# A pre-norm linear-attention block on one core: the weights' opening in smaller pieces, and masks ahead of statistics in the last tiles

## What is computed

```python
x = x + attn(layernorm(x))       # 16 heads of 32
x = x + ffn(layernorm(x))        # 512 -> 512, operands rounded to fp8

# attn: q, k, v = split(x @ W_attn + b_attn);  q, k = elu(.) + 1
kv   = kv + k[:, None] * v[None, :]      # running sums over the tokens
ksum = ksum + k
y    = (q @ kv) / (q . ksum + 1e-6)
out  = y @ W_proj + b_proj
```

## Time and profile before

| | |
|---|---|
| median of 3 runs | 949.95 us (949.16, 949.95, 952.21) |
| profiled execution | 948.85 us, its span 947.1 us |
| PE busy | 918.2 us (97% of the span) |
| ACT busy | 745.6 us (79%) |
| DVE busy | 731.8 us (77%) |
| POOL busy | 641.3 us (68%) |
| granted clock of PE, mean | 0.999 |

### The profile page before, as it was taken

How to read it: one execution, slowest core, us unless ns; L and a number is a source line. 1 busy time by engine, 2 the same in 40 slices (tenths; PEclk the granted TensorE clock), 3 DMA queues, 4 the chain that set the end, 5 groups by cost and what they waited for, 6 DMA issues and landing times.

```text
span 947.1 us, 44776 instructions
## 1 busy us (share of the span) xinstructions
PE 918.2 (97%) x19470; PEld 490.5 (52%) x19532; DVE 731.8 (77%) x1404; ACT 745.6 (79%) x1358; POOL 641.3 (68%) x713
## 2 busy tenths in 40 slices
PE   5998999999999999999999999999999999999896
PEld 2455555555555555555555555555555555555454
DVE  6999879787777777778687687777778687676687
ACT  5788787877869688787877868788787878868874
POOL 5659877766767677676776667677676676764433
PEclk9999999999999999999999999999999999999999
DMA  8926564565464554565555465555555455462421
GB/s 268 143 41 109 109 119 103 97 119 97 95 122 100 98 116 104 96 114 105 95 114 107 91 116 106 89 118 108 92 114 112 89 114 110 90 103 59 76 69 59
DMA packets 252036, 99.12 MB, mean 105 GB/s; under 512 B 232384, under 2 KB 232640, under 8 KB 251840
## 3 DMA queue, kind: packets, MB, share of 16 engines
q1 hardware_dynamic: 251840, 96.25, 52.3%
HBM read 22.81 MB, written 16.78 MB: 42 GB/s over the span
## 4 chain that ended last, share of the span: by engine, by line
PE 90%; POOL 3%; issue 2%; ACT 2%; DVE 2%; SPq 1%; DMA 1%; ACTq 0%; POOLq 0%
PE R L235 77%; PE S L235 13%; POOL st L1029 1%; POOL xn L1031 1%; DMA x2t<-x2b 0%; ACT raw L477 0%; POOL xs L1076 0%; PE R L239 0%; DVE raw L739 0%; POOL raw L1062 0%; DMA xs<-in_L_attn_x 0%; ACT ktok L477 0%; SPq L1227 0%; DVE v L728 0%; ACT o L477 0%
## 5 line engine op out<-in xcount | busy, mean ns | idle before, releaser
L235 PE MATMUL R<-xt,wh 128*128 128x512 f16 x1024 | 306.2, 381 | 2.4 <-ACT wh L477 2.4
L716 DVE SCALAR_TENSOR_TENSOR qk<-qk,rel 128x512 f32<-128x512 f32 x128 | 112.8, 884 | 118.1 <-ACT rel L489 118.1
L477 ACT ACTIVATE raw<-qk 64x512 f32<-64x512 f32 x256 | 160.8, 628 | 48.9 <-PE S L235 45.7
L235 PE MATMUL R<-xt,wl 128*128 128x512 f16 x512 | 194.0, 380 | 0.0
L1083 POOL TENSOR_TENSOR yhl<-y,yhl 128x512 f16<-128x512 f32 x60 | 70.0, 1167 | 146.1 <-ACT yhl L477 146.1
L235 PE MATMUL R<-wh,xt 128*128 128x512 f16 x512 | 158.0, 379 | 0.0
L235 PEld LDWEIGHTS R<-xt,wh 128*128 128x128 f16 x1024 | 96.7, 98 | 116.0 <-DVE xt L882 2.6
L739 DVE TENSOR_TENSOR raw<-S,causal 64x1024 f32<-64x1024 f32 x128 | 155.9, 1218 | 0.9
L1029 POOL TENSOR_TENSOR st<-st,half 128x1 f32<-128x1 f32 x127 | 92.7, 730 | 90.6 <-DVE st L705 89.8
L235 PE MATMUL R<-wph,yt 128*128 128x512 f16 (+1 forms) x520 | 132.4, 377 | 3.9 <-ACT yt L477 1.9
L486 ACT ACTIVATE qk<-R,bqk,wm 128x512 f32<-128x512 f32 x128 | 98.9, 773 | 35.6 <-PE R L235 35.0
(11 more groups left out here) (108 smaller groups left out, 1364.8 us busy)
## 6 DMA issues: line engine op xcount, KB each, us to landing
xs<-in_L_attn_x SPq DMA_DIRECT2D x64, 256.0 KB, 3.1
out<-xs SPq DMA_DIRECT2D x63, 256.0 KB, 2.4
raw<-in_L_attn_W_attn SPq DMA_DIRECT2D x3, 1024.0 KB, 9.5
xs<-in_L_attn_W_proj SPq DMA_DIRECT2D x4, 256.0 KB
raw<-in_L_ffn_weight SPq DMA_DIRECT2D x1, 1024.0 KB, 17.0
raw<-raw SPq DMA_TRANSPOSE x63, 3.7
x2t<-x2b SPq DMA_TRANSPOSE x62, 2.5
xt<-xnhl SPq DMA_TRANSPOSE x60, 3.5
```

What stands on the lines that cost most here:

```text
L235: return e.matmul(out, a, b, start=start, stop=stop, skip_group_check=True)
L477: return e.activation(out, in_, ACT.Copy, **more)
L716: e.scalar_tensor_tensor(qk[j % 2][:, i, :], qk[j % 2][:, i, :], 1.0, rel[:, (u - 1) % 2, :], ALU.min, ALU.add).then_inc(s_phi, 1)
```

## The change

It has an opening part and an ending part. `W_attn` comes in four pieces instead of three (columns 0 to 256, 256 to 512, 512 to 1024, 1024 to 1536), each with its own size, spread and scale; `wh` and `wl` are made in eight parts, the first four of 128 columns. PE runs 16, 3 and 4 transposes that nobody reads (`warm`) among the first tiles' transposes, and `most(1)` inside the first product. `v_peak`, `v_scale`, `proj_scale`, `proj_weight` and `ffn_round` come later in the programs; `ffn_sum` moves from DVE to POOL; `add_bp` of tiles 8 to 23 moves, two at a time, to tiles 8 to 15. In the last tiles DVE makes `update` and the mask ahead of `ln2`, its residual `ffn` comes one tile later, POOL's `spread` comes ahead of `proj`, and PE's `ffn(28)` and `proj(30)` stand otherwise around `values(31)`.

```diff
+PIECES = ((0, 256), (256, 512), (512, 1024), (1024, 1536))
+PARTS = ((0, 128), (128, 256), (256, 384), (384, 512), (512, 768), (768, 1024), (1024, 1280), (1280, 1536))
...
# PE
                     if i == j == 0 and m == 8:
+                        most(1)
                         pe.wait_ge(s_wl, 1)
...
-            for m in range(4):
-                t1(m)
+            warm(16)
+            t1(0)
+            t1(1)
+            warm(3)
+            t1(2)
             most(0)
+            t1(3)
+            warm(4)
             for i in range(12):
                 proj_qkv(0, i)
-                if i in (0, 2, 11):
-                    most((0, 2, 11).index(i) + 1)
+                if i in (1, 4, 11):
+                    most((1, 4, 11).index(i) + 2)
...
                     if n == NT - 1:
-                        proj(n - 1, 0, 4)
+                        ffn(n - 3)
                     values(n)
...
                 if n == NT - 1:
-                    proj(n - 1, 4, 12)
+                    proj(n - 1, 0, 8)
                     t_y(n)
+                    proj(n - 1, 8, 12)
...
-                elif 2 <= n < NT - 1:
+                elif 2 <= n < NT - 2:
                     ffn(n - 2)
# ACT
             t1(1)
+            attn_size(0)
             t1(2)
-            attn_size(0)
             t1(3)
             attn_weight(0)
             attn_weight(1)
             attn_size(1)
-            phi(0, 0)
+            attn_size(2)
             attn_weight(2)
             attn_weight(3)
+            phi(0, 0)
+            attn_weight(4)
             phi(0, 1)
+            attn_weight(5)
...
                     if n == 0:
                         spread(n)
-                        proj_weight()
...
                     values(n)
                     if n == 0:
+                        proj_weight()
                         ahead(chunks(n)[1])
# DVE
             t1_parts(1)
+            scale(0)
             t1_parts(2)
-            scale(0)
             t1_parts(3)
             attn_weight(0)
             attn_weight(1)
-            v_peak()
             scale(1)
-            ln1(4)
-            attn_weight(2)
-            phi(0, 0)
-            attn_weight(3)
+            attn_weight(2)
+            attn_weight(3)
+            scale(2)
+            phi(0, 0)
+            ln1(4)
+            attn_weight(4)
             ln1(5)
             phi(0, 1)
-            scale(2)
+            v_peak()
+            attn_weight(5)
             phi(0, 2)
+            scale(3)
...
+            attn_weight(7)
             ln1(7)
...
             phi(0, 7)
+            v_scale()
             v_out(0, 0)
...
             update(0)
-            proj_scale()
...
+                    if n == 1:
+                        proj_weight()
+                        ahead(chunks(0)[1])
                     if n + 8 < NT:
                         ln1(n + 8)
                     if n == 0:
-                        proj_weight()
+                        proj_scale()
                     if n == 1:
-                        ffn_sum(0, 2)
+                        ffn_round()
...
                 if 1 <= n < NT:
                     proj(n - 1)
                 if n == NT - 1:
+                    ffn(n - 3)
                     t_y(n)
+                if n + 1 < NT and tail(n + 1):
+                    update(n + 1)
+                    scores(n + 1)
                 if 1 <= n < NT:
                     ln2(n - 1)
...
-                elif 2 <= n < NT - 1:
+                elif n < NT - 1 and tail(n - 1):
+                    ffn(n - 3)
+                elif n >= 2 and not tail(n):
                     ffn(n - 2)
# POOL, tile n
+            def ffn_sum(f):
+                pool.wait_ge(s_wfd, 3)
+                e.tensor_tensor(w_b[:, f, :], w_hi[:, f, :], w_lo[:, f, :], ALU.add).then_inc(s_wfs, 1)
...
+                    elif n < 8:
+                        add_bp(n)
+                    elif n < 16:
+                        add_bp(2 * n - 8)
+                        add_bp(2 * n - 7)
...
+                    if n == 1:
+                        ffn_sum(0)
+                        ffn_sum(1)
                     if n:
                         values(n)
+                    if n == 1:
+                        ffn_sum(2)
+                        ffn_sum(3)
+                if n + 1 < NT and tail(n + 1):
+                    spread(n + 1)
...
# SP
-                if n == 1:
-                    t_wf(0)
-                    t_wf(1)
                 if n + 2 < NT:
                     t_k(n + 2)
                 if n % 4 < 3 and n + 8 < NT:
                     t1(n + 8)
                 if n == 1:
+                    t_wf(0)
+                    t_wf(1)
                     t_y(n)
```

More of the change, by code:

```diff
@@ L141, in build @@
         Y = S[:, :, 4 * HALF:4 * HALF + 4 * W]
-        UN = [wm[:, 7 * i + 4:7 * i + 5] for i in range(4)]
-        UP = [wm[:, 7 * i + 5:7 * i + 6] for i in range(4)]
-        UN_V, UN_P = wm[:, 33:34], wm[:, 34:35]
+        UN = [wm[:, 7 * i + 4:7 * i + 5] for i in range(5)]
+        UP = [wm[:, 7 * i + 5:7 * i + 6] for i in range(5)]
+        UN_V, UN_P = wm[:, 41:42], wm[:, 42:43]
         raw_p = xs[:, NX - 4:NX, :]
@@ L162, in build @@
         s_out = [sem(f"xo{i}") for i in range(NX)]
-        s_wa = [sem(f"wa{i}") for i in range(3)]
+        s_wa = [sem(f"wa{i}") for i in range(4)]
         s_wf, s_wp, s_bqk, s_bva, s_bias = sem("wf"), sem("wp"), sem("bqk"), sem("bva"), sem("bias")
@@ L187, in build, with weights @@
         s_rs1, s_xn, s_rs2, s_x2, s_xb, s_x1b = sem("rs1"), sem("xn"), sem("rs2"), sem("x2"), sem("xb"), sem("x1b")
-        s_yl, s_blank, s_one, s_khl, s_near = sem("yl"), sem("blank"), sem("one"), sem("khl"), sem("near")
+        s_wfs, s_yl, s_blank, s_one, s_khl, s_near = sem("wfs"), sem("yl"), sem("blank"), sem("one"), sem("khl"), sem("near")
         bank = {}
+        def weights(first, end):
+            third, at = divmod(first, D)
+            return raw[:, third, :, at:at + end - first]
         def four(t):
@@ L500, in proj_size @@
                 act.wait_ge(s_wp, 64)
-                e.activation(wpl[:, :, :].bitcast(BF16), raw_p, ACT.Abs, accum_out=wm[:, 21:22]).then_inc(s_size, 1)
+                e.activation(wpl[:, :, :].bitcast(BF16), raw_p, ACT.Abs, accum_out=wm[:, 28:29]).then_inc(s_size, 1)
             def attn_weight(i):
[L504 to L507, removed]
+                piece = piece_of(PARTS[i][0])
+                act.wait_ge(s_up, piece + 1)
+                copy(wh[:, :, slice(*PARTS[i])], weights(*PARTS[i]), scale=UP[piece]).then_inc(s_wh, 1)
             def proj_weight():
-                act.wait_ge(s_up, 4)
-                copy(wph[:, :, :], raw_p, scale=UP[3]).then_inc(s_wph, 1)
+                act.wait_ge(s_up, 5)
+                copy(wph[:, :, :], raw_p, scale=UP[4]).then_inc(s_wph, 1)
             def ffn_half():
-                act.wait_ge(s_wl, 4)
+                act.wait_ge(s_wl, part_of(7) + 1)
                 act.wait_ge(s_wfc, 4)
@@ L933, in ffn_round @@
                                 saturate=False).then_inc(s_wfd, 1)
-            def ffn_sum(first, end):
-                dve.wait_ge(s_wfd, 3)
-                for f in range(first, end):
-                    e.tensor_tensor(w_b[:, f, :], w_hi[:, f, :], w_lo[:, f, :], ALU.add).then_inc(s_wfd, 1)
             e.memset(pair[:, :], 0.0).then_inc(s_pair, 1)
@@ L998, in _ @@
                         ffn_high()
-                        ffn_round()
-                        ahead(chunks(n)[1])
                 if 1 <= n < NT:
@@ L1008, in _ @@
                     last_proj()
-                if n + 1 < NT:
+                if n + 1 < NT and not tail(n + 1):
                     update(n + 1)
-                    if tail(n + 1):
-                        scores(n + 1)
-                if n == 1:
-                    ffn_sum(2, 4)
                 if n == NT:
@@ L1143, in _ @@
             ln1(4)
+            ln1(5)
             ln1_parts(4)
-            ln1(5)
             ln1_parts(5)
@@ L1173, in _ @@
                         ln1_parts(n + 8)
+                    if n == 1:
+                        ffn_sum(0)
+                        ffn_sum(1)
                     if n:
                         values(n)
-                    if 1 <= n < 8:
-                        add_bp(n)
+                    if n == 1:
[3 more added lines that the diff above has]
+                    spread(n + 1)
                 if n == NT:
@@ L1182, in _ @@
                     proj(n - 1)
-                if n + 1 < NT:
+                if n + 1 < NT and not tail(n + 1):
                     spread(n + 1)
                 if n == 0:
-                    add_bp(n + 8)
                     add_bp(n)
```

90 lines of the change are left out of this document (44 added, 46 removed).

## The result

The changed kernel takes **969.0 us** (median of 4, 967.37 to 970.25) where the kernel before takes 950.7 (4 runs beside it, 949.16 to 952.21): ratio 1.019, 95% interval 1.0176 to 1.0204. It is 18.3 us slower; the forecast was 947.2, with a range up to 949.8 and a chance of 0.06 for slower. The profiled execution took 967.37, its span is 965.6, so 18.5 us more than before.

A forecast was written before the change was run, and what follows sets the result against it. PE bounds the steady tiles, with DVE deciding in the opening. Gains of 0.7 (opening), 0.2 (after update(0)) and 1.7 (last tiles) make 2.6: 948.85 becomes 946.25, as a median 947.2, range 944.2 to 949.8.

The forecast's parts named there:

- rival 1: Opening: the clock doesn't rise for transposes, so update(0) comes at 52.2; 0.4 gained, 949.5 us; chance 0.20.
- the terms given, 3.0 + 2.0 - 0.3: Opening, PE's second product: earlier start, faster first product from the risen clock, less the second spread waiting inside it.
- the 0.7: Opening: DVE decides when update(0) starts, 50.0 against 50.70, so 0.7 us gained of five.
- rival 3: Opening: POOL becomes the bound through its fp8 sums; at 2.7 us each the time is 953.5; chance 0.06.
- The 50.0: Opening: predicted update(0) time, from 12.3 plus 33.9 of DVE work plus 3.8 of DVE idle time.
- The step that failed: Last tiles: with the residual one tile later, DVE no longer waits for ACT's o; 1.5 us gained.
- The prediction's own sign of being wrong: Last tiles: the forecast is wrong if PE waits for x2t in tiles 28 to 30 by its numbering.
- Rival 4: Last tiles: the end gives nothing, late x2 costing what the masks gain; 949.0 us; chance 0.09.
- the lower bound of this part: Last tiles: a gain of 0 instead of 1.7 us, if late x2 makes PE wait for ffn in each tile.
- From `update(0)` to 90.94: First tiles after update(0): moved weight work on ACT, DVE and POOL; 0.2 us gained, between -1.1 and +0.9.
- the two waits said to cancel there: After update(0): a new PE wait of 1.2 on ACT's relu against the 1.22 wait for y at 76.87 going.
- 0.35 over three tiles: Last tiles: ACT's `k_tokens` comes behind the later x2 and delays PE's update, costing 0.35 us over three tiles.

The follow-up runs named there:

- e2_ending: The kernel before with only the change's new order of the last tiles, its opening as before: 966.08 us, ratio 1.0161 to the kernel before.
- e3_queue: The whole changed kernel, with SP issuing the transposes of normalized tiles 59 to 61 ahead of the stores of tiles 58 to 60: 957.28 us, ratio 1.0067.
- e4_residual: The whole changed kernel, with DVE's residual in the last tiles back at its old place, a tile earlier: 958.20 us, ratio 1.0073 to the kernel before.
- e5_bank: The changed opening with the old last tiles, the projection weight's sum written into unused scores banks instead of the ring: 954.93 us, ratio 1.0043.
- e8_both: The whole changed kernel with the opening mended and SP's last transposes ahead of the stores: 954.56 us, ratio 1.0034 to the kernel before.
- the mended opening: Changed opening, old last tiles; sum's bank moved, projection weight behind phi(1,2), POOL's norm and spread and SP's x2 transpose ahead of ffn-weight work: 950.08 us, ratio 0.9994.

## Why the prediction was wrong

**Right.** The steady tiles moved nothing. The clock rises for transposes alone (rival 1 falls); first product at 12.89 for 13.2; second at 15.70 for 16.0 (the terms given, 3.0 + 2.0 - 0.3, make 16.3); `update(0)` held by DVE at 50.12 for 50.0, so 0.6 for the 0.7; a wait on ACT's relu of 1.12 for 1.2; on x2t of 1.14 for 1.05; POOL's sums at 1.07 each for 1.16 (rival 3 falls). In the end no wait on o by DVE and `last_proj` held by DVE for 1.17, for 1.2.

Two of these hits are in part luck. The 50.0 was added up from 33.9 us of DVE's work and 3.8 of idle time; from 12.3 to 50.05 DVE was busy 32.07 and idle 5.7, so the two errors cancel (the longest single wait, for ACT's relu at 40.64, was 2.71 for 2.0). And the wait on x2t has the right size only because PE and the tile were both late by some 2.7 against `update(0)`.

**The step that failed** is in the last tiles: "One tile later the o has long been there: 1.5 gained." The stall of the earlier trace rows did go. But the step priced a moved DVE instruction only where it stood and where it went, on DVE, ACT and PE. The residual has another reader, the store in SP's queue, and that queue is served in order: behind the store stands the transpose that PE's next ffn needs. The term was +1.5 and cost 14.7, with 3.4 more at the low clock. e2_ending shows the place, e3_queue and e4_residual show the cause from its two ends. The prediction's own sign of being wrong, PE waiting for x2t in these tiles, is what the trace shows.
The Trainium skill (DMA: Bandwidth & Descriptors, the anatomy of one DMA) says that a DMA engine waits for no semaphore and that any such wait is done by the issuing sequencer before dispatch. The trace agrees: nothing is issued by SP from 906.9 to 923.5, with a transpose ready since 914.0.
Rival 4 and the lower bound of this part ("the late x2 makes PE wait for ffn in each tile") named the right wait and the wrong reason for it, and so the wrong price: ACT had the tile ready at 914.0, where PE's ffn came up at 919.2 (917.4 without the stall of 1.87) and a transpose takes 2.4 to land; it then lay 10 us in the queue.

**A second step** was left out: in "From `update(0)` to 90.94" `proj_scale` isn't among the moved work, though it frees a bank of PE's ring. That is 1.7 us, and e5_bank shows that the same bank's place in the ring also makes `update(0)` wait for the third tile of v (48.66 without it, 50.42 with it). Of the two waits said to cancel there, the relu's came and y's stayed (0.82 for 1.22 before): the term was +0.2 and measured -2.6 by `ffn(0)` (93.00 - 50.12 = 42.9, before 40.2). A smaller size was off too: `k_tokens` cost PE 0.97 ahead of `update(61)`, where 0.35 over three tiles had been put.

**What stays open**: why the kernels with the new last tiles and the mended queue spread over 7 us and lose some 4 against the old ones (PE's order around `values(63)` is what they share, but it wasn't run by itself), and why one transposed y took twice its time in e5_bank.

## What to carry to other kernels

When an instruction is moved later, list everyone who waits for its result, the DMA queues first, and for each of them what is queued behind the waiting entry; a store that can wait should not stand ahead of a load or transpose that can't. The same holds for a PSUM bank of a ring: the small reader that frees it is part of the path of whoever takes it next. A wait of PE of several us should be priced with the clock it loses, which is read from the next matmuls' durations.

## What the runs showed of the hardware

- Transposes alone brought the clock up: with 23 idle ones among the 16 real ones the first product ran eight matmuls in 1.89 us, without them in 3.57. The Trainium skill (TensorE: Matmul & The Clock Gate, Part 4) says that transposes don't count as activity for the clock as matmuls do; here the measurement says they do.
- In each profiled execution PE stands once or more near the end with no instruction to run and nothing named but "issue": 1.86 us at 891.49 before, 1.87 at 918.91 after, 2.14 in e3_queue, up to 2.92 in e8_both. With the changed opening it falls on the last two matmuls of `scores(62)` in nearly all kernels, with the old one on `values(59)`. Between 110 and 880 us the only one above 0.4 us is one of 0.72 in e2_ending.
- Behind such a stall the clock may fall, and then it costs about as much again: after 2.14 us in e3_queue the stretch from `ffn(59)` to the transposes took 4.92 instead of 3.23; after 1.55 in the mended opening only the first 2.9 us of work ran at half rate; after another 2.14, in e8_both at 915.25, the same stretch took 3.23 and nothing was lost.
